# The last phase's down projection by seven block products instead of eight

## The reference

```python
x = x + 0.5 * ffn(layernorm(x))
x = x + layernorm_affine(z + sum_k eta[k] * m_k)      # z = layernorm(x) @ W.T, m_k a decaying scan of z along the tokens
x = x + 0.5 * ffn(layernorm(x))

def ffn(x):                                           # hidden width 2048
    return (silu(x @ w_gate.T) * (x @ w_up.T)) @ w_down.T
```

## Time and profile before

| | us |
|---|---|
| median of 3 runs | 1021.67 (1021.63 to 1021.7) |
| span of the profiled execution, first to last instruction | 1020.2 |
| TensorE busy | 1014.4 (99%), 4508 records |
| VectorE busy | 671.5 (66%) |
| ScalarE busy | 408.6 (40%) |
| GpSimd busy | 162.5 (16%) |
| granted TensorE clock, mean | 1.000 |

### The profile page before, as it was taken

How to read it: one execution, slowest core, us unless ns; L and a number is a source line. 1 busy time by engine, 2 the same in 40 slices (tenths; PEclk the granted TensorE clock), 3 DMA queues, 4 the chain that set the end, 5 groups by cost and what they waited for, 6 DMA issues and landing times.

```text
span 1020.2 us, 12550 instructions
## 1 busy us (share of the span) xinstructions
PE 1014.4 (99%) x4508; PEld 841.2 (82%) x4508; DVE 671.5 (66%) x1013; ACT 408.6 (40%) x669; POOL 162.5 (16%) x187
## 2 busy tenths in 40 slices
PE   8999999999999999999999999999999999999998
PEld 8888888888888888888888888888888888888887
DVE  7756665598988687857978877786685333333342
ACT  6645446465433622224732363231382322222311
POOL 4123343125300200210430020021040000000000
PEclk9999999999999999999999999999999999999999
DMA  6588877678667555647856764454677565555265
GB/s 206 224 325 318 301 265 253 252 229 272 242 227 231 182 181 167 200 144 236 270 167 230 235 216 150 146 185 141 228 252 225 207 191 193 204 196 190 85 189 187
DMA packets 61710, 217.89 MB, mean 214 GB/s; under 512 B 6352, under 2 KB 15568, under 8 KB 53968
## 3 DMA queue, kind: packets, MB, share of 16 engines
q1 hardware_dynamic: 61072, 216.03, 62.8%
q10 hardware_dynamic: 576, 1.05, 0.3%
HBM read 170.92 MB, written 46.14 MB: 213 GB/s over the span
## 4 chain that ended last, share of the span: by engine, by line
PE 99%; DVE 1%; DMA 0%; POOL 0%; ACT 0%; issue 0%; DVEq 0%; ACTq 0%
PE ps_a L1569 8%; PE ps_a L1571 8%; PE ps_a L1570 8%; PE ps_b L1569 8%; PE ps_b L1571 8%; PE ps_b L1570 8%; PE ps_c L1569 7%; PE ps_c L1571 7%; PE ps_c L1570 7%; PE ps_d L1569 7%; PE ps_d L1571 7%; PE ps_d L1570 7%; PE aux L1569 3%; PE aux L1571 3%; PE aux L1570 3%; PE ps_d L1731 1%
## 5 line engine op out<-in xcount | busy, mean ns | idle before, releaser
L1060 DVE TENSOR_TENSOR tmp<-tmp,ps_c 128x512 f32<-128x512 f32 x59 | 40.4, 685 | 138.9 <-PE ps_c L1571 138.9
L1569 PE MATMUL ps_a<-xt,gu 128*128 128x512 f32 x304 | 118.3, 389 | 0.0
L1570 PE MATMUL ps_a<-xt,gu 128*128 128x512 f32 x304 | 118.3, 389 | 0.0
L1571 PE MATMUL ps_a<-xt,gu 128*128 128x512 f32 x304 | 118.3, 389 | 0.0
L1570 PE MATMUL ps_b<-xt,gu 128*128 128x512 f32 x286 | 111.3, 389 | 0.0
L1571 PE MATMUL ps_b<-xt,gu 128*128 128x512 f32 x286 | 111.3, 389 | 0.0
L1569 PE MATMUL ps_b<-xt,gu 128*128 128x512 f32 x286 | 111.3, 389 | 0.0
L1571 PE MATMUL ps_d<-dn,hid 128*128 128x512 f32 x256 | 99.6, 389 | 0.0
L1569 PE MATMUL ps_d<-dn,hid 128*128 128x512 f32 x256 | 99.6, 389 | 0.0
L1570 PE MATMUL ps_d<-dn,hid 128*128 128x512 f32 x256 | 99.6, 389 | 0.0
L1570 PE MATMUL ps_c<-xt,gu 128*128 128x512 f32 x236 | 91.8, 389 | 0.0
(11 more groups left out here) (207 smaller groups left out, 2113.7 us busy)
## 6 DMA issues: line engine op xcount, KB each, us to landing
dn<-dn_kept SPq DMA_DIRECT2D x112, 512.0 KB, 3.7
gu<-gu_kept SPq DMA_DIRECT2D x46, 1024.0 KB, 5.0
gu<-gu_kept SPq DMA_DIRECT2D x46, 768.0 KB, 5.6
gu_kept<-gu SPq DMA_DIRECT2D x14, 1024.0 KB, 4.4
gu_kept<-gu SPq DMA_DIRECT2D x14, 768.0 KB, 4.2
dn_kept<-dn SPq DMA_DIRECT2D x16, 512.0 KB, 5.1
h_t<-w_ffn_in SPq DMA_DIRECT2D x18, 256.0 KB, 4.8
x_tok<-w_ffn_in SPq DMA_DIRECT2D x18, 256.0 KB, 5.1
```

The costliest lines, as they stand in the source:

```text
L1060: dve.tensor_tensor(dst, u3s(si), p5_bank(si)[:, :], ALU.add).then_inc(c22_done, 1)
L1569: pe.matmul(dst, a_hi, b_hi, start=start, stop=False, skip_group_check=chained)
L1570: pe.matmul(dst, a_hi, b_lo, start=False, stop=False, skip_group_check=chained)
L1571: return pe.matmul(dst, a_lo, b_hi, start=False, stop=stop, skip_group_check=chained)
```

## The change

The last phase computes both tiles' down projection together, as 2x2 blocks: tokens of tile 2 and tile 3 by the two halves of the output features, with even and odd hidden rows as the inner blocks. Seven products of half width (256 columns) take the place of eight.

1. **Phase 0 makes more weights.** For each pair of `w_down` rows GpSimd makes four sums (`t_sums_of`, 4 operations of 128x256), ScalarE and VectorE split them (`t_hi_of`, `t_lo_of`, 128x1024 each) in `zx`, which has one place for them, and SP writes them out (`keep_t`, two DMAs of 512 KB). 8 pairs. `load_dn_raw` now also waits for the sums. In the window of phase 0 `d1_hi(0)` and `d1_hi(1)` wait for the last split (`t_lo`), `d1_hi(2)` and `d1_hi(3)` for the last of these writes (`t_stored`).
2. **Sets of phase 3.** `first_block` takes the place of `down0_begin` and `down0_end`, with six matmuls of 256 columns at each of the same two places. VectorE gets four subtractions or additions for each pair of hidden rows (`s_of`), behind `c11` of each even set.
3. **End of phase 3.** In place of `down1` stand 20 batches (five products Q5, Q6, Q3, Q7, Q4 of four batches, 24 matmuls of 256 columns each), whose operands are split by `stage_hi_of` and `stage_lo_of` (128x1024, 20 each) into the seven places of `xt`. Products add up in PSUM: Q4 goes on in the banks of Q7 and waits until both have been added to x (`block_added`).
4. `dn` is laid out by halves, `[P, DN, 2, 2, HALF]`, in all phases. Matmuls that take a whole row read two runs of 256.

```diff
 def load_dn_raw(h):
     wait(sp, dn_lo, h - 1)
+    wait(sp, t_sums, 4 * (h // 2))
...
+def keep_t(j):
+    sp.wait_ge(t_lo, j + 1)
+    for part in range(2):
+        sp.dma_start(t_kept[j, :, :, part], t_part(part).bitcast(F32)).then_inc(t_stored, 16)
...
     keep_dn(15)
+    keep_t(7)
...
+def t_hi_of(j):
+    act.wait_ge(t_sums, 4 * j + 4)
+    if j == 0:
+        act.wait_ge(plain_done, 8)
+    wait(act, t_stored, 32 * j)
+    act.copy(t_part(0), t_raw(j)).then_inc(t_hi, 1)
...
 def d1_hi(p, m):
-    if m < 4 and p == 0:
-        act.wait_ge(plain_done, 8)
+    if m < 2 and p == 0:
+        act.wait_ge(t_lo, PAIRS)
+    if 2 <= m < 4 and p == 0:
+        act.wait_ge(t_stored, 32 * PAIRS)
...
+def t_sums_of(j):
+    pool.wait_ge(dn_raw_arrived[0], 16 * (j + 1))
+    pool.wait_ge(dn_raw_arrived[1], 16 * (j + 1))
+    wait(pool, t_lo, j - 1)
+    pool.tensor_tensor(t[:, 0, :], b12, b11, ALU.subtract).then_inc(t_sums, 1)
+    pool.tensor_tensor(t[:, 1, :], b22, b12, ALU.subtract).then_inc(t_sums, 1)
...
+def s_of(q):
+    dve.tensor_tensor(s3, first_row(q, 0), tile1_even, ALU.subtract).then_inc(s_step, 1)
+    dve.tensor_tensor(tile1_even, tile1_even, tile1_odd, ALU.add).then_inc(s_step, 1)
+    dve.wait_ge(s_step, 4 * q + 1)
+    dve.tensor_tensor(s2, tile1_odd, s3, ALU.subtract).then_inc(s_step, 1)
+    dve.wait_ge(s_step, 4 * q + 3)
+    dve.tensor_tensor(s4, first_row(q, 1), s2, ALU.subtract).then_inc(s_step, 1)
...
+def add_block(banks, b, tile, half, semaphore, n, added=0):
+    dve.wait_ge(semaphore, n)
+    wait(dve, block_added, added)
+    x = x_tok[:, 4 * tile + 2 * b:4 * tile + 2 * b + 2, half * HALF:(half + 1) * HALF]
+    dve.scalar_tensor_tensor(x, by_half(banks[b][:, :]), 0.5, x, ALU.mult, ALU.add
+                             ).then_inc(block_added, 1)
...
+def first_block(q, odd, b):
+    pe.wait_ge(lo0_ready, 16 * LAST + 2 * q + odd + 1)
+    for t in (2 * b, 2 * b + 1):
+        a = slice(t * P, (t + 1) * P)
+        last = three(unit_half(y_ps if odd else x_ps, t), hid0[:, odd, 0, a], hid0[:, odd, 1, a],
+                     dn[:, n % DN, odd, 0, :], dn[:, n % DN, odd, 1, :], q == 0 and t % 2 == 0,
+                     q == PAIRS - 1, True)
...
+def batch(w, i):
+    pe.wait_ge(dn_loaded[n % DN], 16 * dn_loads(n))
+    pe.wait_ge(stage_lo, m + 1)
+    if i == 0 and w != Q5:
+        pe.wait_ge(block_added, {Q6: 2, Q3: 6, Q7: 8, Q4: 12}[w])
+    for b in range(2):
+        for k in range(2):
+            for t in (2 * b, 2 * b + 1):
+                last = three(unit_half(banks, t), xt[:, op, 0, k, a], xt[:, op, 1, k, a],
+                             dn[:, n % DN, k, 0, :], dn[:, n % DN, k, 1, :],
+                             w == Q5 and i == k == 0 and t % 2 == 0, i == 3 and k == 1, True)
...
     prod6(g)
-    down0_begin(p, si - 2)
+    if p < LAST:
+        down0_begin(p, si - 2)
+    else:
+        first_block((si - 2) // 2, si % 2, 0)
     prod7(g)
...
-    down0_end(p, si - 2)
+    if p < LAST:
+        down0_end(p, si - 2)
+    else:
+        first_block((si - 2) // 2, si % 2, 1)
     prod3(g)
```

More of the change, by code:

```diff
@@ L240, in first_sg, with by_half, t_raw, t_part @@
             return hid1[:, {"11": 8, "21": 9, "12": 10, "22": 11}[name], :]
+        def by_half(row):
+            return row.rearrange("p (a n) -> p a n", a=2)
+        def t_raw(j):
+            r = 4 * (j % 2)
+            return zx_rows[:, r:r + 2, :].rearrange("p r (a n) -> p (r a) n", a=2)
+        def t_part(part):
+            return zx[:, part, 2:4, :].rearrange("p r (a n) -> p (r a) n", a=2)
+        def first_rows(i, odd):
+            if i == 0:
+                return h_t[:, 2 * odd:2 * odd + 2, :]
+            if i == 1:
+                return zw[:, :, :].bitcast(F32) if odd else gb[:, :, :]
+            r = 4 * odd + 2 * (i - 2)
+            return x_tok[:, r:r + 2, :]
+        def first_row(q, odd):
+            return first_rows(q // 2, odd)[:, q % 2, :]
+        def stage_rows(w, i):
+            return {Q5: hid1[:, 4 * i:4 * i + 3:2, :], Q6: zx_rows[:, 2 * i:2 * i + 2, :], Q3: first_rows(i, 1),
+                    Q7: first_rows(i, 0), Q4: hid1[:, 4 * i + 1:4 * i + 4:2, :]}[w]
+        def stage_op(n):
+            return STAGES[n % len(STAGES)]
         def row_x(k, r):
@@ L500, in _ @@
                         load_zw_raw(k - 4)
+                if k >= 4 and k % 2 == 0:
+                    keep_t(k // 2 - 2)
+            keep_t(6)
             sp.wait_ge(dn_stored[0], 16 * 4)
@@ L640, in hi0 @@
                 p, q = g // SETS, g % SETS // 2
-                n = 32 * p + 2 * (q - 1) + odd if q else 32 * (p - 1) + 14 + odd
-                wait(act, d_done, n + 1)
+                if p == LAST and q:
+                    act.wait_ge(first_done, 2 * (q - 1) + odd + 1)
+                else:
+                    n = 32 * p + 2 * (q - 1) + odd if q else 32 * (p - 1) + 14 + odd
+                    wait(act, d_done, n + 1)
                 act.wait_ge(hid21_done if odd else hid11_done, 8 * p + q + 1)
@@ L908, in _ @@
                 g = SETS * p + SETS - 1
+                if p == LAST:
+                    stage_hi_of(0)
+                    hi0(g, 1)
+                    for n in range(1, 20):
+                        stage_hi_of(n)
+                    break
                 d1_hi(p, 0)
@@ L1156, in zw_lo_of, with add_product @@
+            def add_product(w):
+                banks, tile, half, added = {Q5: (z_ps, 3, 1, 0), Q6: (x_ps, 2, 1, 0), Q3: (z_ps, 2, 1, 8),
+                                            Q7: (x_ps, 3, 1, 6), Q4: (x_ps, 3, 0, 0)}[w]
+                add_block(banks, 0, tile, half, bank_done, w + 1, added)
+                add_block(banks, 1, tile, half, batch_done, 4 * w + 4, added)
             def zw_lo_of(j):
@@ L1364, in after_c11 @@
                     gu_lo_a(si + 1)
+                if p == LAST and si % 2 == 0:
+                    s_of(si // 2 - 1)
                 if p in (1, 2):
@@ L1562, in _ @@
                         decays()
-                window(p)
+                if p < LAST:
+                    window(p)
+            stage_lo_of(1)
+            s_of(PAIRS - 1)
+            stage_lo_of(2)
+            for b in range(2):
+                add_block(x_ps, b, 2, 0, first_done, 2 * PAIRS - 1)
+            stage_lo_of(3)
+            for b in range(2):
+                add_block(y_ps, b, 2, 0, first_done, 2 * PAIRS, b + 1)
+            stage_lo_of(4)
+            for n in range(5, 20):
+                stage_lo_of(n)
+                if n % 4 == 1:
+                    add_product(n // 4 - 1)
+            add_product(Q4)
         @block.tensor
@@ L1876, in _ @@
                     down1(p, m)
+            for odd in range(2):
+                first_block(PAIRS - 1, odd, 0)
+                first_block(PAIRS - 1, odd, 1)
+            for w in (Q5, Q6, Q3, Q7, Q4):
+                for i in range(4):
+                    batch(w, i)
 def kernel(**inputs):
```

170 lines of the change are left out of this document (146 added, 24 removed).

## The result

The change is slower: 1028.01 us median (1026.75 to 1028.88, 4 runs), against 1021.65 (1021.6 to 1021.7, 4 runs) for the kernel before on the same chip. The ratio is 1.0061, 95% interval [1.0049, 1.0074], or +6.4 us. The forecast was 1022.9 with a range up to 1026.3, so the result lies outside it. The profiled execution is the fastest of the four, 1026.75 us with a span of 1025.0. That the runs of the change differ by 2.1 us, where those of before differ by 0.1, is a finding of its own.

The account below looks back on a forecast made before the run. TensorE, busy 99%, was taken to bound the kernel. Terms -6.4 + 3.5 + 1.05 + 2.8 + 0.3 = +1.25 took the median from 1021.67 to 1022.9 us, range 1019.8 to 1026.3.

Parts of the forecast that it names:

- Matmuls: Last phase's down projection: 672 matmuls of 256 columns replace 384 of 512, saving 6.4 us.
- The wait behind prod6: 14 sets of phase 3: TensorE waits before prod7 for ScalarE's copy, 0.25 each, +3.5 us (2.4 to 4.8).
- Q7 to Q4: End of program: Q4 waits until Q7's banks are added to x, +1.05 us (0.9 to 1.2).
- The window of phase 0: Phase 0's window: late stores delay VectorE's list, so TensorE waits for splits, +2.8 us (1.8 to 4.3).
- The slack: Phase 0's window: VectorE's split for down1(14) ends 0.84 us before TensorE needs it, subtracted from the list's delay.
- The 0.64 at `down0(15)`: Phase 0's window: 0.6 us of TensorE's wait might come earlier, at down0(15), with `hi0` behind `d1_hi(0)`.
- Sets of phase 0: Phase 0's sets: added work and writes fit, tightest in set 4, +0.3 us taken.
- set 4's store: Phase 0, set 4: ScalarE waits for `keep_t(0)` behind a 1 MB load, 0 to 1.5 us, 0.3 taken.
- The stores land late, and it is slower: Stores delay `d1_hi(2)` in phase 0's window and `t_hi_of` in earlier sets: +3.9 us, 1025.5; chance 0.37.
- narrow matmuls don't cost their weight load: Last phase's down projection: the rival had each narrow matmul pay its weight load, +48 us, about 1071; chance 0.01.
- a figure of 358 GB/s for a core: Phase 0's sets: this skill estimate would add some 2 us; the forecast set it aside, citing 382 measured.

Follow-up runs that it names:

- last_phase_mended: Seven products alone, no block sums made in the first phase, whole blocks between second and third product, last product released by halves: 1016.20 us, ratio 0.9945 against before.
- whole_block: The change with both halves of the first tile's block between second and third product of a set: 1025.10 us, ratio 1.0035 against before.
- last_phase_only: The last phase's seven products alone, no block sums made, split or stored, kept blocks read instead: 1021.29 us, ratio 0.9995 against the kernel before.
- q4_halves: The change with the last product's first two units released after the first bank's addition, the others after the second's: 1027.79 us, ratio 1.0064 against before.
- copy_before_silu: The change with ScalarE's third-bank copy put ahead of the silu in the first full set: 1028.51 us, ratio 1.0069 against before.
- all_second: The change with whole blocks, split last product, earlier stores, the window's second reordering and the copy ahead of the silu: 1016.92 us, ratio 0.9954 against before.
- t_store_earlier: The change with each store of block sums issued in the set that makes them, one set earlier: 1027.39 us, ratio 1.0055 against before.

## Why the prediction was wrong

The mechanisms were the ones named; four of the five waits lay where the text put them. It failed by sizes, all in one direction, and by one wait that it didn't name. Against the forecast span of 1021.5 the profiled one is 3.5 longer: 1.5 from the wait behind prod6, 1.2 from the window, 0.9 from the sets of phase 0. The other 1.3 of the median's excess is in runs without a profile.

- **Matmuls, -6.4.** Right. The narrow ones run at 0.120 in 20 batches without a gap between them but for the one from Q7 to Q4, and last_phase_mended brings 5.5 with 0.6 of it lost again.
- **The wait behind prod6, +3.5.** Right place and cause, shown by whole_block. This term was mis-sized: it measured 5.0, above the upper bound of 4.8 (4.5 in last_phase_only, q4_halves and copy_before_silu). The wait was 0.18 as worked out. The first matmul after it cost 0.11, not 0.07, and I had taken the restart as over after one matmul, while the ten after it were slower too, 0.06 more in most sets. Narrow blocks without a wait cost 0.03 to 0.04 a set too (whole_block, all_second), and no term held that.
- **Q7 to Q4, +1.05.** Right (1.1), shown by q4_halves. Inside it one part was off: TensorE starts 0.15 after VectorE's addition ends (1009.77 to 1009.92), where the sum took the 0.05 of ScalarE.
- **The window of phase 0, +2.8.** The chain was right, this term was mis-sized: 4.0, and up to 4.6 in the other kernels with the same order (4.8 in whole_block, with the clock's 1.6 in it). The store landed 5.8 us after its issue and not 5.0, which is 0.8. VectorE, 5.25 late at its normed row, was 5.54 late at the window's last splits, which is 0.3, and the restarts after the waits make the rest. That the store was issued at 208.44 and not 207.5 comes from the sets, whose loss had made TensorE 0.9 late too, so it adds nothing here. The slack was as summed: 5.54 less 0.84 is 4.7, and TensorE leaves the window 4.9 later than before, with those 0.9 in it. The 0.64 at `down0(15)` was named with its size, but it comes from VectorE's eighth split and not from `hi0` behind `d1_hi(0)`.
- **Sets of phase 0, +0.3.** This step failed. I gave set 4's store 0 to 1.5, and in the profiled runs it is 0.3 to 2.6, with the clock's 1.6 behind it in the worst. The row that should have set the bound was in the text: a load of 1 MB in that very place took 7.6 us to land, and this store, issued right behind it, took 8.5 in the change and up to 10.0 elsewhere (whole_block). And for GpSimd I counted only whether its own time fits into a set, not what it does to VectorE beside it. That is the gap in set 2, 0.8 us, which no term held.
- **The rivals.** "The stores land late, and it is slower" came true in its outcome and in its second place, ScalarE's `t_hi_of` in set 4. In the window the last store landed 5.8 us after its issue, the very edge of its condition, and 6.0 to 6.5 in the other kernels that issue its two parts together. Its 1025.5 took 7.6 there, which none reached: it was too dear in the window and still too low, since the sets cost more than it held. That narrow matmuls don't cost their weight load is confirmed.
- **Of memory bandwidth** the forecast kept its sum against a figure of 358 GB/s for a core. A stretch of 3 us above moved 433 GB/s. all_second's fourth slice moved 382 over 25 us, and TensorE had no gap in it. The Trainium skill ("Perfetto Trace Analysis", Roofline, the note on more than 100%) calls 358 the share when both cores of a pair are at work, and puts the limit of one core alone at its DMA engines, some 435. The rows agree with that.

What stays open: why the first pair's store lands 8.5 us after its issue in one profile and 10.0 in another, when those of the next pairs take 5.4 to 6.9. That it stands behind a load of 1 MB is in the order; that this load is the cause no run shows, since t_store_earlier moves the store away from the load and from the busiest stretch together (in the change the share of the DMA engines is 0.57 from 53 to 60 us and 1.05 from 64 to 73). That the median's last 1.3 us lie in set 4 as well is argued, not shown.

## What to carry to other kernels

When a kernel runs one engine without a gap, price a change by the covers that it thins: work that is made narrower also covers less, and here seven products that save 6.4 us gave 0.6 until a half block was made a whole one at each copy. A wait in a list costs its length plus a slow restart, and everything queued behind it moves by the same amount, so order the list by what is needed first and put waits for stores last. And a buffer that must be stored before it is used again wants its store issued in the set that fills it, with well over the median landing time to spare (here the median was 5.8 us and the worst 10.0).

## What was not expected of the hardware

- A wait of 0.18 us in TensorE's list cost 0.31 to 0.35: the first matmul after it takes 0.11 more, and the ten after it together 0.02 (all sets of last_phase_only, three of the change) or 0.06 (the change's other 11). What decides between the two no run shows. Without the wait, mixing 256 and 512 columns costs 0.03 to 0.04 a set.
- After standing 2.3 us TensorE went on at the 1.2 GHz level for eight matmuls (0.427 apart, granted clock 0.57 over four microseconds), 1.6 us more. In whole_block the same followed a gap of 2.2 us from start to start in the window, and did not follow one of 2.1 in set 4.
- GpSimd beside VectorE's operations with two inputs in SBUF: 0.74 became 1.7 us for the one, 0.68 became 1.23 and 2.35 became 3.45 for the other.
- VectorE's end reached TensorE after 0.14 to 0.15 us (209.65 + 0.68 to 210.48, 1009.08 + 0.69 to 1009.92), ScalarE's after 0.05 (862.41 + 0.59 to 863.05).
